# Attention heads on TensorE: the probability-value products written two steps at a time

## What is computed

```
x = x + conv_attention(group_norm(x))     # 8 heads of 16 channels, 1024 x 1024 softmax per head and image
x = x + conv_next(group_norm(x))          # 7x7 depthwise conv, LayerNorm, 128 -> 512 GELU -> 128

attn = softmax(einsum('bgdi,bgdj->bgij', q, k) * SCALE)
out  = einsum('bgij,bgdj->bgdi', attn, v)
```

## Time and profile before

| | us |
|---|---|
| median of three runs | 379.86 (379.63 to 380.43) |
| span of the profiled execution | 375.1 |
| TensorE busy | 324.2 (86%) |
| VectorE busy | 261.6 (70%) |
| ScalarE busy | 194.0 (52%) |
| GpSimd busy | 104.5 (28%) |

### The profile page before, as it was taken

How to read it: one execution, slowest core, us unless ns; L and a number is a source line. 1 busy time by engine, 2 the same in 40 slices (tenths; PEclk the granted TensorE clock), 3 DMA queues, 4 the chain that set the end, 5 groups by cost and what they waited for, 6 DMA issues and landing times.

```text
span 375.1 us, 5651 instructions
## 1 busy us (share of the span) xinstructions
PE 324.2 (86%) x2072; PEld 115.7 (31%) x2072; DVE 261.6 (70%) x269; ACT 194.0 (52%) x359; POOL 104.5 (28%) x137
## 2 busy tenths in 40 slices
PE   7987987999998069999999999998993689876696
PEld 3643612233332013333333333332320234321242
DVE  3736374889898017778856889888799335999920
ACT  1423044777775027777775656666673255553132
POOL 5410101011101001100110105799993010695610
PEclk9858559999999559999999999999997699989999
DMA  5156847000069920000000000095000000871001
GB/s 193 28 187 106 114 63 120 3 29 30 2 124 125 123 25 1 2 2 1 3 0 2 2 1 3 24 220 114 2 1 2 0 0 2 218 156 48 0 0 56
DMA packets 10880, 19.97 MB, mean 53 GB/s; under 512 B 1892, under 2 KB 2789, under 8 KB 10853
## 3 DMA queue, kind: packets, MB, share of 16 engines
q1 hardware_dynamic: 10856, 19.64, 26.4%
HBM read 13.61 MB, written 5.54 MB: 51 GB/s over the span
## 4 chain that ended last, share of the span: by engine, by line
PE 66%; DVE 14%; DMA 11%; issue 4%; POOL 2%; ACT 2%; SPq 1%; DVEq 0%; ACTq 0%; POOLq 0%
PE ps L962 15%; PE ps L921 15%; PE ps L951 12%; DVE qs L740 6%; DMA qs<-mrows 6%; PE ps L1108 3%; DVE mx L692 3%; PE ps L1042 3%; PE ps L884 3%; PE ps L871 2%; DMA ks<-parts_dram 2%; PE ps L883 2%; DMA xr<-pad_dram 2%; PE ps L1122 2%; PE ps L942 2%
## 5 line engine op out<-in xcount | busy, mean ns | idle before, releaser
L692 DVE TENSOR_REDUCE mx<-ps 128x1 f32<-128x1024 f32 x128 | 154.3, 1220 | 63.3 <-PE ps L921 58.9
L566 ACT ACTIVATE pr<-ps 128x512 f32<-128x512 f32 x256 | 139.0, 595 | 97.9 <-PE ps L951 97.6
L951 PE MATMUL ps<-qs,ks 99*128 99x512 bf16 x256 | 79.4, 388 | 17.1 <-DMA qs<-mrows 16.3
L921 PE MATMUL ps<-ks,qs 96*128 96x512 bf16 x256 | 81.2, 404 | 6.3 <-DVE mx L692 3.7
L962 PE MATMUL ps<-pr,va 128*32 128x256 f32 x1024 | 83.1, 397 | 0.0
L740 DVE SCALAR_TENSOR_TENSOR qs<-xpad,w,qs 128x512 f32<-128x512 f32 (+1 forms) x35 | 54.3, 1551 | 1.0
L438 POOL TENSOR_TENSOR mparts<-zeros,mx 128x8 bf16<-128x8 f32 x16 | 3.7, 231 | 179.4 <-DVE mx L692 179.4
L951 PEld LDWEIGHTS ps<-qs,ks 99*128 99x128 bf16 x256 | 24.4, 99 | 60.6 <-DMA qs<-mrows 16.8
L962 PEld LDWEIGHTS ps<-pr,va 128*32 128x32 f32 x1024 | 20.3, 108 | 51.0 <-issue 46.4
L921 PEld LDWEIGHTS ps<-ks,qs 96*128 96x128 bf16 x256 | 16.6, 99 | 53.4 <-issue 39.7
L1042 PE MATMUL ps<-xr,wt 128*32 128x512 f32 x224 | 28.1, 628 | 3.2 <-DMA xr<-pad_dram 3.2
(11 more groups left out here) (98 smaller groups left out, 257.5 us busy)
## 6 DMA issues: line engine op xcount, KB each, us to landing
parts_dram<-part SPq DMA_DIRECT2D x12, 256.0 KB, 2.7
xr<-pad_dram SPq DMA_DIRECT2D x8, 361.0 KB, 6.1
qs<-parts_dram SPq DMA_DIRECT2D x6, 256.0 KB, 11.5
ks<-parts_dram SPq DMA_DIRECT2D x6, 256.0 KB, 16.3
xr<-pad_dram SPq DMA_DIRECT2D x4, 304.0 KB, 10.5
qs<-parts_dram SPq DMA_DIRECT2D x6, 192.0 KB, 4.9
ks<-parts_dram SPq DMA_DIRECT2D x6, 192.0 KB, 7.8
xr<-pad_dram SPq DMA_DIRECT2D x4, 285.0 KB, 10.7
```

The costliest lines, as they stand in the source:

```text
L566: nc.scalar.activation(pr[:, j % PR, c * HALF:(c + 1) * HALF], st[c], ACT.Exp, scale=SCALE).then_inc(exp_done, 1)
L692: nc.vector.tensor_reduce(mx[:, r, i:i + 1], sm[i % 2], AX.X, ALU.max).then_inc(max_done, 1)
L921: last = nc.tensor.matmul(sm[i % 2][:, c * HALF:(c + 1) * HALF], qs[0:STACK, bass.ds(s * N + i * P, P)], ks[0:STACK, bass.ds(s * N + c * H ...
L951: nc.tensor.matmul(st[c], ks[0:ROWS, bass.ds(t * N + j * P, P)], qs[0:ROWS, bass.ds(t * N + c * HALF, HALF)], start=True, stop=True).then_ ...
```

## The change

At even steps TensorE's list now holds the products of the two steps before, one behind the other; at odd steps it holds none. At step 0 these are the last two products of the head before, and the last two of head 15 follow behind its loop. Nothing is changed on the other engines, and the number of instructions is the same.

```diff
@@ head(t, r, turn, also), TensorE
                     scores_t(t, j)
-                    if j:
-                        times_v(t, r, j - 1)
-                    elif t:
-                        times_v(t - 1, 1 - r, NT - 1)
+                    if j % 2 == 0:
+                        for n in range(2):
+                            if j:
+                                times_v(t, r, j - 2 + n)
+                            elif t:
+                                times_v(t - 1, 1 - r, NT - 2 + n)
                     if j == turn:
                         turn_max(t + 1, 1 - r)
@@ behind head 15
+            times_v(T - 1, 1, NT - 2)
             times_v(T - 1, 1, NT - 1)
```

## The result

The changed kernel takes 388.46 us (384.76 to 391.4, 4 runs), the kernel before 379.75 (377.3 to 380.43, 4 runs): a ratio of 1.0234, 95% interval 1.0167 to 1.0300. A second measurement, on another chip, gave 387.30 us against 379.70, 1.0233 (1.0171 to 1.0295). It is slower by 7.6 to 8.7 us, and both intervals lie above 1; 390.8 had been forecast, in a range of 385.5 to 397.

What follows compares the result with a forecast made beforehand. TensorE was taken to set the pace, ScalarE's exponentials close behind; with pairs they bind. The stretches 3.0 + 3.1 + 0.9 - 0.3 + 2.4 + 0.9 + 0.9 sum to +10.9 us: 379.86 becomes 390.8 us, range 385.5 to 397.

Steps and rivals of the forecast that it cites:

- E: The second `scores_t` matmul of a pair's even step, forecast 1.57 us (1.64 in the loop) behind the odd step's first matmul.
- first rival: Attention heads: exponentials don't bind, TensorE's 2.87 us sets the pair, 373 us in all; chance 0.05.
- price of a pair: Two steps of a head: 3.37 us, or 3.44 in loop heads 2 to 7, against 3.08 before.
- second product: Eight matmuls directly behind another product call at even steps: 0.46 us, between 0.44 and the 0.57 of a lone call.
- heads 5 to 8: h5 s2 to h8 s0, eleven loop pairs: +3.1 us; head 8: +0.9 us.
- heads 10 and 11: Eight pairs of 3.37 instead of 3.08 us, and `scores` twice at step 7: +2.4 us.
- Head 9: First pair loses 0.3 us, everything after step 5's projection starts 0.5 sooner: -0.3 us, between -0.6 and +0.3.
- The stalls: DMA waits at h5 s0 and h14 s0: only a later issue counts; h5 s0 moves +3.0 us, waiting some 13 us.
- the rival in which the stalls take the loss: h5 s0 and h14 s0 land by their own clock, so only about +0.9 us stays; chance 0.03.
- h0 s4 to h5 s0: Twelve pairs to h3 s4 add 2.4 us, the copy of head 4's maxima 0.6: h5 s0 moves by +3.0 us.
- the clock falls: Small idle gaps lower TensorE's clock for a third of the pairs: +25 us, 415 us in all; chance 0.04.
- The tail: Head 15 behind step 2: two second products on the chain, ahead of `ln_var` and `copy_u`, cost +0.9 us.

Runs made afterwards that it cites:

- second profile: The kernel before, profiled again with no edit: 379.68 us, a span of 377.9 us where its first profile had 375.1.

## Why the prediction was right

**Direction and mechanism: right.** Every step of the argument about the loop through `st` has its row: the wait is at E, for L566, once a pair; leaving out half of the exponentials turns the loss into a gain; emptying the other step of work makes the same loss without touching the products; filling the odd step brings the pair to 2.97 us. The first rival (faster, the exponentials don't bind) is what the half-exponential version shows: it decides at 1.1 us behind the odd step's first matmul, and 1.21 was enough for 374 us.

**The price of a pair: 0.05 us too high.** Forecast 3.37 and 3.44, measured (as a head's quarter) 3.32 and 3.38. The second product costs 0.43, not 0.46, a little below the bound of 0.44 from the convolution; E to the products was as taken. From one E to the next the loop heads take 3.40 us three times and 3.32 once (s2 to s4), head 8 takes 3.32 to 3.33. Over 39 pairs that is 2 us: heads 5 to 8 lost 3.1 where 4.0 was forecast, heads 10 and 11 2.0 instead of 2.4.

**Head 9: right.** -0.6 against -0.3: the bound of -0.6 was reached.

**The stalls: right about the issue, wrong about the stall, short in the size.** The fetches were issued at 111.69 us instead of 106.64, and h5 s0 moved with them, which rules out the rival in which the stalls take the loss. But the stall was to shrink to some 13 us, and it took 14.81 (14.16 and 14.61 in the two profiles of the kernel before). From its own start head 4 came to the wait only 0.5 us later, not 1.5; one product more of it now stands behind the wait. And from the issue of the fetches to h5 s0 it took 29.3 us instead of 28.2 and 28.6; no run shows why. Over h0 s4 to h5 s0 the loss was 4.4 to 4.8 us against the second profile, not 3.0. Of it 1.8 to 2.2 us lie between h0 s4 and h1 s0, where two pairs should have cost 0.6. That step of the forecast failed: it priced head 0 at full clock. The window from 60 to 72 us, in the changed kernel and in the kernel before again (columns as in the earlier trace rows):

```profile
60.00:72.00 12.00, 8.61 (x50) 2.77 (x51) 4.52 (x5) 4.01 (x9) 1.67 (x6) 0.72 0.29 58
```

```profile
60.00:72.00 12.00, 9.40 (x81) 2.90 (x73) 7.73 (x7) 7.00 (x15) 1.68 (x6) 1.00 0.25 55
```

The granted clock is 0.72 there and was 1.00: it fell to the level of 1.2 GHz at 61.4 us, while TensorE waited for `ks` at h0 s3, and stayed there for 6.8 us. The rows of that wait, in the same order:

```profile
63.35 1.01 PE L921 MATMUL ps<-ks,qs 96*128 96x512 bf16 x2 [3.77 <-DMA ks<-parts_dram]
```

```profile
62.96 0.59 PE L921 MATMUL ps<-ks,qs 96*128 96x512 bf16 x2 [2.60 <-DMA ks<-parts_dram]
```

In this profile TensorE stands for 3.77 us instead of 2.60. But the length of the wait doesn't decide it: the changed kernel profiled again waited 2.45 us there and still had a low-clock window of 3.4 us. All eight profiles of kernels with pairs in head 0 have a low-clock window of 3.4 to 6.8 us there. Of the five with single products in head 0, three have none (one of them, with the scores alone moved, waits only 0.85 us there) and two have one of 3.4 us. So the order may make it likelier and is not alone in causing it; neither is shown, and the cause stays open.

What it costs can be read. From h0 s4 to h1 s0 it takes 6.20 us with single products and a granted clock of 1.00, 7.71 and 7.78 with single products and the low-clock window of 3.4 us (half the exponentials in the kernel before; pairs in heads 5 to 13), and 8.01 with pairs and a window of the same length. So about 1.5 us belong to the clock and 0.2 to 0.3 to the two pairs.

The clock did fall, but not where the rival "the clock falls" had it: in the steady heads, with waits of half a microsecond in 3.4, the granted clock was 1.00 from 147 to 270 us.

**The tail: wrong.** +0.9 was forecast. From h15 s3 to the end the changed kernel took 79.7 and 79.8 us, the kernel before 78.0 and 79.8, and undoing the change in head 15 gave nothing. The term counted the two products that come later (1.1 to 1.2 us) and not the one that leaves step 3 (1.1 at the low clock there); what is left is smaller than what the low-clock windows there move from run to run (1.8 us).

**The sum.** Against the second profile of the kernel before, the span grew by 9.9 us, and 10.9 was forecast; against the medians it is 7.6 to 8.7. The tail (-1), the pair (-2), head 0 (+2), the time from the issue of the fetches to h5 s0 (+0.7) and heads 9 and 12 to 14 (-1.2) make up the difference within a microsecond. So part of the agreement is luck: the head 0 that was missed made up for pairs and a tail that were priced too high.

## What to carry to other kernels

When an engine's list is regrouped, don't ask only what the group saves on its own engine: go round the buffer's loop, and count for each step what stands between two uses of the same buffer. Two banks of PSUM give the reader just one step of cover, so work has to be even over the steps; a regrouping pays only if something else fills the step that it empties, and here the two moves are a loss of 2.3% and of 3.3% alone and still of 1.7% together, and they came out about even only after `normalise` or one scores tile was put elsewhere and some heads were left as they were. After each such move look for the next wait that was just hidden before: here VectorE's normalising, then GpSimd's split.

## What had not been expected of the hardware

- A second call of eight f32 products in four groups of 32 columns costs 0.43 us behind its like and 0.57 alone (1.00 us for the 16, from 174.14 to 175.14 us). So about 0.14 us is saved on leaving the narrow groups; on the way in the difference is 0.1 (0.33 us from `scores_t` to the products, 0.22 to another full-width matmul).
- Two profiles of one program differ by 2.8 us in their span (375.1 and 377.9 us) with every step of heads 6 to 8 the same to 0.01 us; most of the difference goes with the places and lengths of the low-clock windows at the end, and with the landing of the fetches.
